# AdaLN block with deformable attention and an 8-expert layer: another order on ScalarE, and the masks before the last three images

## What is computed

```python
mod = (silu(c) @ wmod).reshape(16, 6, 1, 128)      # sa, ca, ga, sb, cb, gb; |ga|, |gb| at least 0.25
h = layernorm(x) * (1 + ca) + sa
# attention: 33 samples per row at positions pos = row + s * freq + phase, s = -16..16
wave = silu(h @ wave_w.T + wave_b)                  # gives one freq and one phase per row
w = silu(h @ kernel_w.T + kernel_b)                 # 8 heads x 33 weights per row
out[l] = sum_s w[l, s] * lerp(h, pos[l, s])         # pos clipped to 0..255
x = x + ga * silu(out @ out_w.T)
h = layernorm(x) * (1 + cb) + sb
mask = one_hot(top_2(h @ router_w.T + router_b))    # 8 experts
x = x + gb * (sum_e mask_e * (h @ expert_w[e]) + mask @ expert_b)
```

## Time and profile before

| | before |
|---|---|
| median of three runs | 292.21 us (292.1 to 293.36) |
| the profiled execution | 291.6 us, its span 289.8 us |
| mean granted TensorE clock | 0.988 |
| PE busy | 263.6 us, 91% |
| DVE busy | 259.2 us, 89% |
| ACT busy | 228.0 us, 79% |
| POOL busy | 40.2 us, 14% |
| chain that ended last | ACT 32%, DVE 31%, PE 24%, issue 11% |

### The profile page before, as it was taken

One profiled execution on the slowest core, in us unless ns is written; L12 is line 12 of the kernel. 1 busy time (PEld: TensorE's weight loads), 2 busy tenths in 40 slices (PEclk: granted clock), 3 DMA queues, 4 the chain that ended last, 5 costly groups with the idle time before them and its releaser, 6 DMA issues.

```text
span 289.8 us, 5448 instructions
## 1 busy us (share of the span) xinstructions
PE 263.6 (91%) x1884; PEld 182.7 (63%) x1884; DVE 259.2 (89%) x543; ACT 228.0 (79%) x641; POOL 40.2 (14%) x61
## 2 busy tenths in 40 slices
PE   7999886999889998999899998999999989999895
PEld 3444642874567476866587477837884778487664
DVE  7989999998969998999989998999999999973462
ACT  4885899599978998899979998899779767655310
POOL 4203402300410022000200012002400300040100
PEclk9999998699999999999999999999999999999999
DMA  6550000020002000050005000500041004100101
GB/s 180 195 129 0 0 0 0 2 66 1 1 0 119 31 1 0 3 163 3 0 1 165 0 0 2 160 8 1 2 104 62 1 0 118 49 2 0 38 0 54
DMA packets 11869, 12.08 MB, mean 42 GB/s; under 512 B 1014, under 2 KB 10818, under 8 KB 11842
## 3 DMA queue, kind: packets, MB, share of 16 engines
q1 hardware_dynamic: 11398, 11.33, 13.0%
q10 hardware_dynamic: 444, 0.40, 0.5%
HBM read 9.59 MB, written 2.14 MB: 40 GB/s over the span
## 4 chain that ended last, share of the span: by engine, by line
ACT 32%; DVE 31%; PE 24%; issue 11%; POOL 1%; ACTq 0%; DVEq 0%; POOLq 0%
DVE AT L847 13%; ACT A L519 6%; DVE T L814 5%; ACT xn L383 4%; PE pT L1066 4%; ACT xn L417 4%; ACT c L502 3%; PE pE L1151 3%; PE pY L1151 2%; PE pL L1117 2%; PE pR L1066 2%; ACT u L484 2%; ACT T L453 2%; ACT hT L440 2%; PE pR L1043 1%
## 5 line engine op out<-in xcount | busy, mean ns | idle before, releaser
L814 DVE COPY_PREDICATED T<-mask,T 128x1472 f32<-128x1472 int16 (+9 forms) x54 | 76.6, 1418 | 0.5
L847 DVE TENSOR_TENSOR AT<-T,c 128x2064 f32<-128x2064 f32 x32 | 72.4, 2305 | 0.0
L519 ACT ACTIVATE A<-pT 128x512 f32<-128x512 f32 x64 | 35.1, 603 | 27.6 <-PE pT L1066 27.0
L1151 PE MATMUL pE<-hm,late 128*128 128x256 f32 x196 | 47.0, 387 | 0.0
L1151 PEld LDWEIGHTS pE<-hm,late 128*128 128x128 f32 x196 | 35.8, 190 | 5.9
L1066 PE MATMUL pT<-first,AT 128*128 128x128 f32 x256 | 34.6, 279 | 3.2 <-DVE AT L857 3.1
L519 ACT ACTIVATE A<-pR 128x512 f32<-128x512 f32 x64 | 35.5, 622 | 0.3 <-PE pR L1066 0.3
L322 POOL TENSOR_SCALAR ve<-sq 128x4 f32<-128x4 f32 (+1 forms) x14 | 9.9, 710 | 185.3 <-ACT xn L383 185.3
L1066 PEld LDWEIGHTS pT<-first,AT 128*128 128x128 f32 x256 | 29.4, 144 | 9.2 <-DVE AT L857 7.7
L1066 PE MATMUL pR<-first,AT 128*128 128x128 f32 x256 | 33.9, 276 | 0.0
L1080 PE MATMUL pY<-A,hs 128*32 128x256 f32 x512 | 32.4, 383 | 0.3
(11 more groups left out here) (153 smaller groups left out, 403.1 us busy)
## 6 DMA issues: line engine op xcount, KB each, us to landing
mkb<-mask_rows SPq DMA_DIRECT2D x6, 896.0 KB, 5.0
x<-in_x SPq DMA_DIRECT2D x7, 256.0 KB, 5.7
out<-x SPq DMA_DIRECT2D x7, 256.0 KB, 5.0
late<-in_late SPq DMA_DIRECT2D x1, 592.0 KB, 3.8
mkb<-mask_rows SPq DMA_DIRECT2D x1, 448.0 KB, 3.5
x<-in_x SPq DMA_DIRECT2D x2, 128.0 KB, 3.5
wmod<-in_wmod ACTq DMA_DIRECT2D x1, 256.0 KB, 4.4
out<-x SPq DMA_DIRECT2D x2, 128.0 KB, 3.2
```

The source lines that it names most:

```text
L519: nc.scalar.activation(A[b][:, m, 2 * j:2 * j + 2, :].rearrange("p h l -> p (h l)"), four_banks(k)[:, :], ACT.Copy).then_inc(a_A, 1)
L814: nc.vector.copy_predicated(rows[:, :, :, j0:j1], spread(mask[:, k, 0:w, j0:j1], [P, w, H, j1 - j0], 2), rows[:, :, :, j0 + (1 << bit):j1 ...
L847: nc.vector.tensor_tensor(cells_of(bt).rearrange("p h (j r) -> p h j r", r=BLK), spread(T[n % 2][:, bt, 0:H, 0:NB], [P, H, NB, BLK], 3), s ...
L1151: ins = mm(dst, weT[:, e, :], hm[b][:, e, :], start=False, stop=(e == EM - 1))
```

## The change

On ScalarE, in the loop, `front_fall(i)` goes from ahead of the fourth `front_row` to behind `stats2(i - 1)`. `norm2(i - 1)` goes ahead of `sums1(i + 2)`, and `back_h2T(i - 1)` goes ahead of `front_u(i + 1)` and `squares1(i + 2)`. At i = 7 `back_mk(6)` goes between the two halves of `mid_A(7)`'s first image, on ScalarE and on TensorE. In the tail `back_moe(6)` goes ahead of `mid_A(8)`.

On GpSimd `expert_weights` goes away. It is on VectorE now, at i = 1 behind the last network stage, and `selectors` goes to the same place of i = 0. In VectorE's tail both `masked(6, ...)` stand among the last network stages of unit 8, `total(6)` stands ahead of `masked(7, 0)`, and a wait for g_rs2 is gone.

On TensorE `back_plain` runs once a unit, over all its columns, and waits for a_mk first. The second image's experts are split around `back_x2T`. The four warm-up matmuls behind `back_x2T` stay at i = 1 and 2 only. In the tail the experts of unit 6 all stand ahead of `mid_A(8)`, and the warm-ups are 8 and 4 where they were 5 and 6. SyncE reads unit 6's masks back in two halves, each with its semaphore.

```diff
@@ SyncE, masks(n) @@
-                sp.dma_start(mkb[n % 2][:, :, 0:w], spread(scratch[n % 2][:, 0:w], [P, EM, w], 0)).then_inc(d_mkb[n % 2], 16)
+                parts = ((0, L, d_mkb[n % 2]), (L, w, d_mkl)) if n == LATE - 1 else ((0, w, d_mkb[n % 2]),)
+                for c0, c1, landed in parts:
+                    sp.dma_start(mkb[n % 2][:, :, c0:c1],
+                                 spread(scratch[n % 2][:, c0:c1], [P, EM, c1 - c0], 0)).then_inc(landed, 16)
@@ GpSimd, the loop @@
                 run(i, -1, rstd2)
                 run(i, 2, rstd1)
-                if i == 0:
-                    expert_weights()
@@ ScalarE, the loop @@
                 run(i, 1, front_row, 2)
-                run(i, 0, front_fall)
                 run(i, 1, front_row, 3)
                 run(i, 1, front_wave)
...
                 run(i, -1, stats2)
+                run(i, 0, front_fall)
                 if i >= 0:
                     run(i, 1, front_hs)
+                run(i, -1, norm2)
                 run(i, 2, sums1)
+                run(i, -1, back_h2T)
                 run(i, 1, front_u)
-                run(i, -1, norm2)
                 if i < 0:
                     run(i, 1, front_hs)
                 run(i, 2, squares1)
-                run(i, -1, back_h2T)
                 run(i, -2, back_moe)
-                run(i, 0, mid_A, 0)
-                run(i, -1, back_mk)
+                run(i, 0, mid_A, 0, (0,))
+                if i == LATE:
+                    back_mk(LATE - 1)
+                run(i, 0, mid_A, 0, (1,))
+                if i < LATE:
+                    run(i, -1, back_mk)
@@ VectorE, masked(n, b) @@
+                elif n == LATE - 1:
+                    dve.wait_ge(d_mkl, 16)
@@ VectorE, the loop @@
                 run(i, 0, network, range(5, 6))
+                if i == 0:
+                    selectors()
+                elif i == 1:
+                    expert_weights()
...
                     gates()
-                    selectors()
@@ TensorE, back_plain @@
-                mm(dst, weT[:, EM, :], h2T_of(n)[:, b * L:(b + 1) * L], start=True, stop=False)
-                if b == 0:
-                    pe.wait_ge(a_mk, n + 1)
-                mm(dst, ebp[:, :], mkT_of(n)[:, b * L:(b + 1) * L], start=False, stop=False)
...
+                pe.wait_ge(a_mk, n + 1)
+                w = tiles(n) * P
+                mm(moe_bank(n)[:, 0:w], weT[:, EM, :], h2T_of(n)[:, 0:w], start=True, stop=False)
+                mm(moe_bank(n)[:, 0:w], ebp[:, :], mkT_of(n)[:, 0:w], start=False, stop=False)
@@ TensorE, the loop @@
                 run(i, -2, back_experts, 0)
-                second(i, -2, back_experts, 1)
+                second(i, -2, back_experts, 1, range(0, 2))
...
                 run(i, -1, back_x2T)
-                if i > 0:
+                second(i, -2, back_experts, 1, range(2, EM))
+                if 0 < i < 3:
                     warm_up(4, pT[0])
```

More of the change, by code:

```diff
@@ L350, in rstd2 @@
                 rstd(n, ve2, rs2, g_rs2, mu2, nm2, g_nm2)
-            def expert_weights():
-                pool.wait_ge(d_late, 32)
-                nc.gpsimd.tensor_tensor(weT[:, 0:EM, :], weT[:, 0:EM, :], spread(weT[:, EM, :], [P, EM, C], 1),
-                                        ALU.subtract).then_inc(g_we, 1)
-                pool.wait_ge(g_we, 1)
-                nc.gpsimd.tensor_scalar(weT[:, EM, :], weT[:, EM, :], 2.0, None, ALU.mult).then_inc(g_we, 1)
             for i in range(-2, NU + 2):
@@ L616, in _ @@
             mid_gate(LATE)
+            back_moe(LATE - 1)
             mid_A(LAST, 0)
@@ L674, in selectors, with expert_weights @@
                 nc.vector.tensor_copy(sel[:, :, :], spread(ident[0:NP * E, 0:EM], [NP * E, EM, P], 2)).then_inc(v_ebp, 1)
+            def expert_weights():
+                dve.wait_ge(d_late, 32)
+                nc.vector.tensor_tensor(weT[:, 0:EM, :], weT[:, 0:EM, :], spread(weT[:, EM, :], [P, EM, C], 1),
+                                        ALU.subtract).then_inc(v_we, 1)
+                dve.wait_ge(v_we, 1)
+                nc.vector.tensor_scalar(weT[:, EM, :], weT[:, EM, :], 2.0, None, ALU.mult).then_inc(v_we, 1)
             def modulation(part):
@@ L970, in _ @@
             sum_ends(LAST, 1)
-            network(LAST, range(2, 6))
             masked(LATE - 1, 0)
+            network(LAST, range(2, 4))
+            masked(LATE - 1, 1)
+            network(LAST, range(4, 6))
             spread_out(LAST, 0)
@@ L977, in _ @@
             stats2(LATE)
-            dve.wait_ge(g_rs2, LATE + 1)
-            masked(LATE - 1, 1)
             route(LATE)
@@ L1144, in back_experts @@
                 img = before(n) + b
-                dst = moe_bank(n)[:, b * L:(b + 1) * L]
                 if own[0] == 0:
-                    back_plain(n, b, dst)
+                    if b == 0:
+                        back_plain(n)
+                    if n < LATE:
+                        pe.wait_ge(v_hm, img + 1)
                 for e in own:
@@ L1150, in back_experts, with back_plain @@
                         pe.wait_ge(v_hm, masked_before(img) + e // 2 + 1)
-                    ins = mm(dst, weT[:, e, :], hm[b][:, e, :], start=False, stop=(e == EM - 1))
+                    ins = mm(moe_bank(n)[:, b * L:(b + 1) * L], weT[:, e, :], hm[b][:, e, :], start=False,
+                             stop=(e == EM - 1 and b == UNITS[n][1] - 1))
                 if own[-1] == EM - 1:
                     ins.then_inc(t_moe, 1)
-            def back_plain(n, b, dst):
-                if b == 0:
-                    if n == 0:
-                        pe.wait_ge(v_ebp, 8)
-                        pe.wait_ge(g_we, 2)
-                    if n == LATE:
-                        pe.wait_ge(v_x2, NU)
-                    elif n == LAST:
-                        pe.wait_ge(v_out, LATE)
-                    elif n > 0:
-                        pe.wait_ge(v_out, n)
-                mm(dst, weT[:, EM, :], h2T_of(n)[:, b * L:(b + 1) * L], start=True, stop=False)
-                if b == 0:
-                    pe.wait_ge(a_mk, n + 1)
-                mm(dst, ebp[:, :], mkT_of(n)[:, b * L:(b + 1) * L], start=False, stop=False)
-                if n < LATE:
-                    pe.wait_ge(v_hm, before(n) + b + 1)
+            def back_plain(n):
+                if n == 0:
+                    pe.wait_ge(v_ebp, 8)
+                    pe.wait_ge(v_we, 2)
+                if n == LATE:
+                    pe.wait_ge(v_x2, NU)
+                elif n == LAST:
+                    pe.wait_ge(v_out, LATE)
+                elif n > 0:
+                    pe.wait_ge(v_out, n)
+                pe.wait_ge(a_mk, n + 1)
+                w = tiles(n) * P
+                mm(moe_bank(n)[:, 0:w], weT[:, EM, :], h2T_of(n)[:, 0:w], start=True, stop=False)
+                mm(moe_bank(n)[:, 0:w], ebp[:, :], mkT_of(n)[:, 0:w], start=False, stop=False)
             def back_out(n):
@@ L1221, in _ @@
             mid_attend(LATE, 1, 1)
[L1223 removed]
+            back_experts(LATE - 1, 0, range(0, 4))
             mid_y(LATE)
[L1225 to L1226 removed]
+            back_experts(LATE - 1, 0, range(4, EM))
             mid_gate(LATE)
[L1228 removed]
+            back_experts(LATE - 1, 1)
+            warm_up(8, pT[0])
             mid_A(LAST, 0, 0)
             mid_A(LAST, 0, 1)
+            back_out(LATE - 1)
             mid_attend(LAST, 0, 0)
             mid_attend(LAST, 0, 1)
[L1233 removed]
             back_x2T(LATE)
             mid_y(LAST)
[L1236 removed]
             back_logits(LATE)
             mid_gate(LAST)
[L1239 removed]
+            warm_up(4, pT[0])
             back_mk(LATE)
[L1241 removed]
             back_mb(LATE, 0)
[L1243 removed]
             back_experts(LATE, 0, range(0, 4))
```

16 lines of the change are left out of this document (3 added, 13 removed).

## The result

The changed kernel takes **299.09 us** (median of six runs, 296.56 to 301.46), the kernel before 292.15 us in the same session: a ratio of 1.0189, interval 1.0135 to 1.0244. It is slower, where I forecast 288.2 us. The profiled execution is the fastest of the six, 296.56 us with a span of 294.8 against the 289.8 of before, so the trace shows 5.0 us of loss and not the whole.

The account below looks back on a forecast made before the run. VectorE was taken to bound the kernel. Start -1.35, loop -3.0 and tail +0.3 sum to -4.05 us, from 292.21 to 288.2 us; range 287.2 to 289.0, chance 0.45.

Parts of the forecast that it names:

- What bounds the kernel: Loop: VectorE is nearly full, busy 29.74 of 30.9 us an iteration; only its waits can be won.
- ScalarE's order, i = 3 to 5: Loop: the new ScalarE order removes VectorE's waits for the logits, 1.15 + 0.92 + 0.92 = 3.0 us won.
- rival (a): Loop: GpSimd's nm meets prodN and comes 1.0 us later, so uR holds VectorE; 290.1 us, chance 0.18.
- The margin at uR: Loop, i = 3 to 5: uR is ready 0.3 us before VectorE asks for it.
- i = 2: Loop, i = 2: waits of 2.83 and 0.83 not won; a 3.3 us wait at uR replaces one, net 0.
- Start: i = 0 to 2: moving expert_weights and selectors to VectorE, with TensorE's clock staying up, wins 1.35 us.
- the case I named for a clock that falls all the same: Start, i = 1: TensorE's clock still drops, so the start wins only 0.7 us or a little less.
- Tail: After the loop: unit 8's transposes 2.9 us later, part comes back; net +0.3 us, between +2.2 and -1.6.
- my bound of +2.2: Tail: the upper limit given for the tail's loss, 2.2 us.
- I take half, 1.8: Tail: of up to 3.75 us, half comes back between unit 8's transposes and the copy of unit 7's masks.
- the plain part: Tail: unit 7's second image no longer has its own plain matmul part, 0.75 us won.
- Rival (e): Loop: fewer warm-ups let TensorE's clock fall; slower from two iterations on, 302.7 us over i = 3 to 7; chance 0.06.

Follow-up runs that it names:

- experiment 4: The changed kernel with the first norm's statistics (sums1, squares1, rstd1) taken one unit further ahead, in double buffers: 292.96 us, ratio 1.0007.
- Experiment 3: The kernel before with three unread memsets on GpSimd ahead of the first norm's variance, nothing else changed: 297.33 us, ratio 1.0205.
- experiment 1: The changed kernel with ScalarE's loop put back in the order of before: 297.2 us, ratio 1.019.
- experiment 2: The kernel before with only ScalarE's loop in the new order: 300.35 us, ratio 1.0291.
- experiment 8: The kernel of experiment 7 plus warm-ups ahead of back_x2T, three at i = 3 to 6 and twelve at i = 7: 287.87 us, ratio 0.9844.
- experiment 9: The kernel of experiment 8 with the change's own tails instead of the old ones: 291.52 us, ratio 0.9982.
- Experiment 12: The kernel before with only expert_weights (i = 1) and selectors (i = 0) moved on VectorE as in the change: 292.48 us, ratio 1.001.
- experiment 5: The changed kernel with VectorE waiting for the first norm's nm ahead of the second image's AT: 295.54 us, ratio 1.0131.
- experiment 6: The changed kernel with the tails of ScalarE, VectorE and TensorE as before: 296.39 us, ratio 1.0119.
- experiment 7: The changed kernel with the first norm's statistics one unit further ahead and the old tails: 289.79 us, ratio 0.9926.
- experiment 10: The changed kernel with the four warm-ups behind back_x2T in every iteration again: 297.96 us, ratio 1.0171.
- experiment 11: The changed kernel plus only warm-ups ahead of back_x2T, three at i = 3 to 6 and twelve at i = 7: 298.86 us, ratio 1.0212.

## Why the prediction was wrong

**What bounds the kernel.** Right. With the collision out of the way the loop runs at 30.0 us with VectorE busy for 29.76 (experiment 4).

**ScalarE's order, i = 3 to 5: -3.0 forecast, +1.3 measured.** The step that failed is this one: "The squares and the experts' output then end near 146.4, before 146.91, when the A copies began". As a statement on ScalarE it was good to 0.2 us: counted from hT, 19.8 forecast and 19.7 measured. But I stopped there. Moving squares1 also moves rstd1 behind it on GpSimd, and so the first norm's nm; I counted no step on GpSimd for it and never asked where VectorE would be. The trace of before had what was needed: nm at 1.33 inside AT the earlier trace rows. I used it for the second norm at i = 2 and in rival (a), and not for the first norm, which the change made meet a run of 5.3 us. Experiment 3 shows the mechanism alone, 1 and 2 that ScalarE's order brings it about, 4 that with the demand moved away i = 3 to 5 take 29.7 to 30.0 us. The kernel of experiment 8 has 29.77, 29.98 and 29.96, 3.2 us less than before together, where I had 3.0.

**The margin at uR** held, but by less than 0.1 us where I gave it 0.3: uR ends at 145.55, as forecast when counted from hT, and VectorE asks for it at 145.59, 0.3 sooner than I had it. eI follows AT without a gap, and rival (a) did not come about at the place that I gave it. Its mechanism did, on another queue.

**i = 2: 0 forecast, +2.0 measured.** The wait at uR is 3.30 us, as worked out. It takes the place of 2.83 at lg, while the residual's wait stays at 0.91 instead of going. The rest is a held rs (6.13 us) in this iteration as well, which I had not counted. In experiment 8, where no one waits for it, i = 2 loses 0.3.

**Start: -1.35 forecast, -0.7 measured.** That is the case I named for a clock that falls all the same: it was low at 52 to 55 us. near at 0.34 and expert_weights at 1.28 are as forecast. In the profiled execution of experiment 9 the clock did not fall at i = 1, and its hT of unit 3 comes at 62.89 us for 64.29: 1.4 sooner, the whole term. Experiment 12 shows that with these two alone even the 0.7 does not arrive.

**Tail: +0.3 forecast, +2.7 measured**, outside my bound of +2.2. From the last hT to the end of unit 7's attention TensorE is 0.3 later. From there to unit 8's transposes it takes 11.1 us for 7.6: 3.5 later and not 2.9, 0.3 of it a wait for y that I had not counted. From those transposes to the copy of unit 7's masks it takes 12.3 for 12.9, so 0.6 comes back, where I had 1.8 ("I take half, 1.8"): this is the term that was mis-sized most. In experiment 9, where the clock stays at its full rate up to the masks' copy, the same stretch takes 11.4, so 1.5 comes back: 0.8 of it also in experiment 8, which keeps the experts there, and 0.7 for moving the experts. The other 0.9 is the clock, which in the change falls at 270.9, ahead of that copy. From the masks to the end 0.6 comes back, for the 0.75 of the plain part. The experts that went had filled TensorE's waits for h2T, hit and mkT. They were cover and not load, and without them TensorE waited where it had worked. The clock then falls in these waits; that was not in my bounds.

**Rival (e)** gave the right sign for another reason. The steady iterations of the change ran at a clock of 1.00 and were long all the same. Falls came at single places, most of them behind a wait of TensorE: at i = 7 in experiments 4 to 7 and 10, in the tail in the change and in 4 and 9 to 11, at i = 5 in 1 and 2, at i = 3 in 3, at i = 2 in the change and in 2 and 4. So the risk I gave 0.06 was real and its place wrong: not the gap of 0.9 that the removed warm-ups left, but, as far as the traces show, above all the waits that open where experts are moved away from ahead of back_x2T or out of the tail's chain. Experiments 2 and 3 have falls too, and there neither experts nor warm-ups were moved. The Trainium skill (TensorE: Matmul & The Clock Gate, HAM oscillation) warns of idle gaps between groups of matmuls. Experiments 7 and 8 agree, with 3.42 us for nine matmuls behind a gap of 2.89 and 2.32 for ten behind one of 0.32. The change's own profiled execution does not: 2.32 for ten behind a gap of 2.88. So a gap of this length lets the clock fall in some executions and not in all.

**Open.** Why rs is caught in one iteration and nm in another is a matter of some tenths, and I did not map where the edge lies. Nor did I try a rstd without two-input instructions on GpSimd. How much of the change's loss is the clock in its typical run is not settled, since the profiled execution was its fastest.

## What to carry to other kernels

Follow a moved step through every engine that its result passes, to the one who waits for it: here 1.4 us of small GpSimd work behind the squares decided, and not the squares. Ask of small GpSimd instructions what VectorE runs at that moment, and either ask for them an iteration later or give them a pause of half a microsecond. Before work is moved ahead of a late chain, look at what it was filling: matmuls between the waits of a dependent chain cost little there (of 3.1 us taken out, 0.7 came back), and TensorE is then not idle in these waits.
